# The last diagonal block of the attention scores: three reduced-precision passes in place of one full-precision matmul

## The reference

```python
qkv = silu(hidden @ qkv_w.T)              # 32 heads, q, k, v of 128 each
scores = einsum('bhnd,bhmd->bhnm', cq, ck) * diag_decay   # within a block of 32
intra  = einsum('bhnm,bhmd->bhnd', scores, cv)
inter  = einsum('bhnd,bhde->bhne', cq * q_decay, kv)      # kv carried from block to block
attn   = intra + inter                    # then RMS norm over all heads * norm_w
out1   = (sigmoid(hidden @ gate_w.T) * normed) @ out_w.T
```

## Time and profile before

| | |
|---|---|
| time, 3 runs | 1119.74, 1120.38 (median), 1122.15 us |
| the profiled execution | 1121.61 us, of which the span of its instructions is 1119.8 us |
| TensorE busy | 1085.3 us, 97% of the span, 5884 matmuls |
| weight loads busy | 944.8 us, 84% |
| DVE, ACT, POOL busy | 717.0, 683.6, 635.0 us (64%, 61%, 57%) |
| mean granted TensorE clock | 0.994 of full speed |

### The profile page before, as it was taken

How to read it: one execution, slowest core, us unless ns; L and a number is a source line. 1 busy time by engine, 2 the same in 40 slices (tenths; PEclk the granted TensorE clock), 3 DMA queues, 4 the chain that set the end, 5 groups by cost and what they waited for, 6 DMA issues and landing times.

```text
span 1119.8 us, 18930 instructions
## 1 busy us (share of the span) xinstructions
PE 1085.3 (97%) x5884; PEld 944.8 (84%) x5884; DVE 717.0 (64%) x1205; ACT 683.6 (61%) x1394; POOL 635.0 (57%) x617
## 2 busy tenths in 40 slices
PE   4999799999999999999999999999999999999997
PEld 3888588988889888988889888988889888888896
DVE  7767375575756667475766757566665757566666
ACT  6667365675656756575656756566566756567530
POOL 5837747376554846367473755458463765548620
PEclk9999899999999999999999999999999999999999
DMA  8213302021111101012020212011010211111122
GB/s 283 65 55 116 120 24 63 19 81 43 48 38 42 61 23 61 19 42 67 28 69 5 80 36 66 19 42 61 23 61 19 76 45 42 43 43 62 52 76 76
DMA packets 42805, 64.23 MB, mean 57 GB/s; under 512 B 3984, under 2 KB 21392, under 8 KB 42512
## 3 DMA queue, kind: packets, MB, share of 16 engines
q1 hardware_dynamic: 42480, 63.73, 17.8%
q10 hardware_dynamic: 288, 0.03, 0.0%
HBM read 54.84 MB, written 8.91 MB: 57 GB/s over the span
## 4 chain that ended last, share of the span: by engine, by line
PE 92%; DMA 2%; DVE 2%; issue 1%; POOL 1%; ACT 1%; SPq 0%; DVEq 0%; ACTq 0%; POOLq 0%
PE bank_q L1751 8%; PE bank_q L1753 8%; PE bank_q L1752 8%; PE bank_r L1752 5%; PE bank_r L1753 5%; PE bank_r L1751 5%; PE bank_p L1751 5%; PE bank_p L1753 5%; PE bank_p L1752 5%; PE outp L1753 5%; PE outp L1752 5%; PE outp L1751 5%; PE score L1753 3%; PE score L1752 3%; PE score L1751 3%; PE att L1753 3%
## 5 line engine op out<-in xcount | busy, mean ns | idle before, releaser
L413 POOL TENSOR_TENSOR w_lo<-combo,w_hi 128x768 fp32r<-128x768 f32 (+1 forms) x128 | 168.0, 1321 | 146.6 <-ACT w_hi L588 146.6
L413 POOL TENSOR_TENSOR w_lo<-raw,w_hi 128x256 fp32r<-128x256 f32 (+1 forms) x128 | 133.2, 1042 | 127.4 <-ACT w_hi L588 127.0
L450 POOL TENSOR_TENSOR sum_sq<-sum_sq,square 128x512 f32<-128x512 f32 x64 | 83.1, 1298 | 93.0 <-ACT square L731 92.9
L1326 DVE TENSOR_TENSOR acc<-acc,outp 128x512 f32<-128x512 f32 x116 | 79.5, 685 | 64.4 <-PE outp L1753 63.1
L1751 PE MATMUL bank_q<-c_hi,w_hi 128*128 128x512 f32 x276 | 110.3, 400 | 5.6 <-ACT ys L588 5.0
L1753 PE MATMUL bank_q<-c_hi,w_lo 128*128 128x512 f32 x276 | 108.9, 395 | 0.0
L1752 PE MATMUL bank_q<-c_lo,w_hi 128*128 128x512 f32 x276 | 108.7, 394 | 0.0
L1236 DVE TENSOR_TENSOR score<-score,table 128x512 f32<-128x512 f32 (+1 forms) x128 | 75.8, 628 | 42.7 <-PE score L1753 42.6
L588 ACT ACTIVATE p_hi<-score 128x896 fp32r<-128x896 f32 (+1 forms) x128 | 81.4, 650 | 35.6 <-DVE score L1236 33.2
L1751 PE MATMUL outp<-wo_hi,g_hi 128*128 128x512 f32 x252 | 100.4, 398 | 1.8 <-DVE acc L1324 1.8
L1184 DVE TENSOR_TENSOR xs<-bank_r,xs 128x512 f32<-128x512 f32 x64 | 44.2, 691 | 89.9 <-ACT xs L588 62.2
(11 more groups left out here) (268 smaller groups left out, 3450.5 us busy)
## 6 DMA issues: line engine op xcount, KB each, us to landing
raw<-w_chunks SPq DMA_DIRECT2D x165, 256.0 KB, 2.9
near_dram<-near SPq DMA_DIRECT2D x2, 2048.0 KB, 8.9
table<-near_dram SPq DMA_DIRECT2D x32, 128.0 KB, 2.0
acc<-x SPq DMA_DIRECT2D x8, 256.0 KB, 5.9
acc<-x SPq DMA_DIRECT2D x2, 1024.0 KB, 6.5
xb_dram<-acc SPq DMA_DIRECT2D x2, 1024.0 KB, 5.0
y<-xb_dram SPq DMA_DIRECT2D x8, 256.0 KB, 3.5
out<-acc SPq DMA_DIRECT2D x8, 256.0 KB, 2.2
```

The source lines that it names most:

```text
L413: pool.tensor_tensor(piece(w_lo[i % 2], j), piece_source(i, j), piece(w_hi[i % 2], j).bitcast(F32), ALU.subtract).then_inc(wlo[j], 1)
L450: pool.tensor_tensor(sum_sq[:, s % 2, :], sum_sq[:, s % 2, :], square[:], ALU.add).then_inc(summed, 1)
L1326: dve.tensor_tensor(tile, tile, outp, ALU.add).then_inc(acc_done, 1)
```

## The change

The scores of block j = 3 are computed by `three` like those of the other blocks, from the last 128 columns of `k_hi`, `k_lo`, `q_hi` and `q_lo`. `k_hi` and `k_lo` grow from 384 to 512 columns, and with them the silu, the high copy and the low subtraction of k. The tiles `q_last` and `k_last` and the instructions that fill them go, on ACT; `whole` remains for v alone, and the wait `scored` moves into `hi`. The order of everything else stays.

```diff
-                k_hi[b] = sb(f"k_hi{b}", [P, K_COLS], F32R, within)
-                k_lo[b] = sb(f"k_lo{b}", [P, K_COLS], F32R, within)
-                q_last[b] = sb(f"q_end{b}", [P, P], at=within)
-                k_last[b] = sb(f"k_end{b}", [P, P], at=within)
+                k_hi[b] = sb(f"k_hi{b}", [P, SEQ], F32R, within)
+                k_lo[b] = sb(f"k_lo{b}", [P, SEQ], F32R, within)
...
-                    cols = slice(0, SEQ if i == V1 or (i != V2 and ROW[c] == 0) else 256 if i == V2 else K_COLS)
+                    cols = slice(0, 256 if i == V2 else SEQ)
...
-                    elif ROW[c] == 1:
-                        made(i, c)
-                        scored(i, b)
-                        act.activation(k_last[b][:], banks[c][:, K_COLS:], ACT.Silu)
-                    else:
-                        act.wait_ge(silued[c], ev(g, i) + 1)
-                        scored(i, b)
-                        copy(q_last[b][:], banks[c][:, K_COLS:])
...
                     else:
+                        scored(i, b)
                         part = (q_hi if ROW[c] == 0 else k_hi)[b][:]
...
-                copy(q_last[b][:], bp[:, K_COLS:])
...
-                act.activation(bq[:, 0:K_COLS], bq[:, 0:K_COLS], ACT.Silu).then_inc(first_silu, 1)
-                act.activation(k_last[b][:], bq[:, K_COLS:], ACT.Silu)
+                act.activation(bq, bq, ACT.Silu).then_inc(first_silu, 1)
...
-                            pe.matmul(score23[:, P_LEN[2]:P_LEN[2] + P], k_last[b][:], q_last[b][:], start=True, stop=True,
-                                      skip_group_check=True).then_inc(s23, 1)
-                        else:
-                            to = score23[:, 0:P_LEN[2]] if j == 2 else score[:, j, 0:P_LEN[j]]
-                            three(to, k_hi[b][:, key], k_lo[b][:, key], q_hi[b][:, j * P:], q_lo[b][:, j * P:],
-                                  j < 2, True).then_inc(s23 if j == 2 else s01, 1)
+                        to = score[:, j, 0:P_LEN[j]] if j < 2 else score23[:, 0:P_LEN[2]] if j == 2 else score23[:, P_LEN[2]:P_LEN[2] + P]
+                        three(to, k_hi[b][:, key], k_lo[b][:, key], q_hi[b][:, j * P:], q_lo[b][:, j * P:],
+                              j != 2, True).then_inc(s01 if j < 2 else s23, 1)
```

More of the change, by code:

```diff
@@ L141, in build @@
         rs = sb("rs", [P, 4, NTB])
-        q_hi, q_lo, k_hi, k_lo, q_last, k_last, y = ([None] * BATCH for _ in range(7))
+        q_hi, q_lo, k_hi, k_lo, y = ([None] * BATCH for _ in range(5))
         for b in range(BATCH):
@@ L627, in whole @@
                     b = COL[c]
-                    if i == V2:
-                        made(i, c)
-                        at_least(act, att_ready, STEPS * (g - 1) + 4 * ROW[c] + 2 + b + 1)
-                        act.activation(v_last[ROW[c], b][:], banks[c][:, 256:512], ACT.Silu)
-                    elif ROW[c] == 1:
-                        made(i, c)
-                        scored(i, b)
-                        act.activation(k_last[b][:], banks[c][:, K_COLS:], ACT.Silu)
-                    else:
-                        act.wait_ge(silued[c], ev(g, i) + 1)
-                        scored(i, b)
-                        copy(q_last[b][:], banks[c][:, K_COLS:])
+                    made(i, c)
+                    at_least(act, att_ready, STEPS * (g - 1) + 4 * ROW[c] + 2 + b + 1)
+                    act.activation(v_last[ROW[c], b][:], banks[c][:, 256:512], ACT.Silu)
                 def hi(i, c):
@@ L785, in body @@
                     copy_u3(QK1)
-                    whole(QK1, "p")
                     weight(QK2, 2)
@@ L790, in body @@
                     silu(QK1, "q")
-                    whole(QK1, "q")
-                    whole(QK1, "x")
                     hi(QK1, "q")
@@ L796, in body @@
                     squares(1)
-                    whole(QK1, "r")
                     copy_m1(QK2)
@@ L810, in body @@
                     copy_u3(QK2)
-                    whole(QK2, "p")
                     weight(G23, 4)
@@ L816, in body @@
                     gated_hi(2)
-                    whole(QK2, "q")
                     silu(QK2, "x")
-                    whole(QK2, "x")
                     hi(QK2, "q")
@@ L831, in body @@
                     copy_u2(G23)
-                    whole(QK2, "r")
                     weight(QK3, 4)
@@ L848, in body @@
                     silu(QK3, "p")
-                    whole(QK3, "p")
                     probs01(4)
@@ L856, in body @@
                     silu(QK3, "x")
-                    whole(QK3, "x")
                     hi(QK3, "x")
@@ L863, in body @@
                     silu(QK3, "q")
-                    whole(QK3, "q")
                     weight(G01, 3)
@@ L868, in body @@
                     copy_m1(QK0)
-                    whole(QK3, "r")
                     weight(G01, 4)
@@ L1023, in body @@
                 silu(QK0, "p")
-                whole(QK0, "p")
                 copy_u3(QK0)
@@ L1030, in body @@
                 gated_hi(6)
-                whole(QK0, "q")
                 hi(QK0, "q")
-                whole(QK0, "x")
                 weight(NEXT + V1, 1)
@@ L1040, in body @@
                 weight(NEXT + V1, 2)
-                whole(QK0, "r")
                 weight(NEXT + V1, 4)
@@ L1088, in first_k @@
                 act.wait_ge(first_ready, TB * b + 2)
-                act.activation(bq[:, 0:K_COLS], bq[:, 0:K_COLS], ACT.Silu).then_inc(first_silu, 1)
-                act.activation(k_last[b][:], bq[:, K_COLS:], ACT.Silu)
+                act.activation(bq, bq, ACT.Silu).then_inc(first_silu, 1)
                 act.wait_ge(first_silu, 2 * b + 2)
-                copy(k_hi[b][:], bq[:, 0:K_COLS]).then_inc(first_high, 1)
+                copy(k_hi[b][:], bq).then_inc(first_high, 1)
             def first_gates(b, h):
@@ L1704, in first_lows @@
                 dve.wait_ge(first_high, 2 * b + 2)
-                dve.tensor_tensor(k_lo[b][:], bq[:, 0:K_COLS], k_hi[b][:].bitcast(F32), ALU.subtract).then_inc(first_low, 1)
+                dve.tensor_tensor(k_lo[b][:], bq, k_hi[b][:].bitcast(F32), ALU.subtract).then_inc(first_low, 1)
             def combo_lo(k, n):
```

## The result

The changed kernel takes 1127.37 us (median of 4 runs, 1126.98 to 1128.47), the kernel before, run beside it, 1121.27 us (4 runs, 1119.74 to 1122.9): a ratio of 1.006, 95% interval 1.0045 to 1.0076. The profiled execution took 1128.47 us, 1126.6 of them its span, so the span grew by 6.8 us. The medians of four grew by 6.1 us; the interval of the ratio allows 5.0 to 8.5.

A forecast was written before the change was run, and what follows sets the result against it. TensorE alone was taken to bound the loop: 0.336 - 0.225 = +0.111 us a step, times 62 steps = +6.9 us, so 1121.61 became 1128.5 us profiled, 1127.3 us as median; range 1119.0 to 1132.0 us.

The forecast's parts named there:

- The bound: Loop on TensorE: busy for all 129.08 us of a period, so only what TensorE gains or loses reaches the total.
- Price of the pass: New 128-column `fp32r` matmuls in the scores: each costs its weight load, 0.112 us, so three cost 0.336 us a step.
- The Trainium skill's 81 ns: Scores on TensorE: 81 ns per load and matmul pair would give +0.018 us a step, +1.1 us in all.
- Price of the old pair: Full-precision matmul removed from the scores: two records by two weight loads, taken as 0.225 us a step.
- Steps that count: Two of 64 steps lie before first-body waits that do not end with them; 62 x 0.111 = +6.9 us.
- the wait for `p_lo` in the last body: TensorE's 0.3 us wait at the end, behind DVE instructions: grows by +0.13 us at most, counted in the range.
- ACT: Copies and silu of q and k on ACT: net -0.35 us a step, -22 us, no effect on the total.
- DVE: Low part of k on DVE: +0.13 us a step, 8.5 us in all, inside 47 us free per period.
- the copy to `ys`: Behind DVE's slowest low part of k (1.80 us): 1.5 us of room before TensorE needs it, enough for 0.6 us more.
- The clock: First body, 126 to 135 us, mean granted clock 0.62: half-clock stretch may shorten or lengthen, about 2 us either way.

The follow-up runs named there:

- e1: Kernel after, with the last score block again by one full-precision matmul, from k_hi and q_hi alone: 1120.77 us.
- e4: Kernel before, with its ACT and DVE work, but the last score block by three reduced passes (stand-in third key block): 1128.45 us.
- e3: Kernel after, with the three passes of the last score block over its upper 64 query columns alone, same three weight loads: 1127.14 us.
- e7: Kernel after without the last block of the scores: 1108.49 us in one run.
- e6: Kernel after with the three passes of the last score block done twice: 1145.78 us in one run.
- e5: Kernel after, with the three narrow passes of the last score block alternating with the three 512-column passes of the first: 1128.69 us.

## Why the prediction was right

- *The bound.* Right. The period grew by what TensorE was given, and e1 and e4 put all of it there.
- *Price of the pass: 0.112 us, from the one-column matmuls of the earlier trace rows.* Right: 0.111, whatever the columns (e3). That the load sets it was my reason, and it is the likely one, not a shown one. The Trainium skill's 81 ns for a pair of load and 128-column matmul (TensorE: Matmul & The Clock Gate, "Back-to-back issue gap") doesn't hold for these `fp32r` operands, which take 111. By the Trainium skill's rule for a load, columns divided by 1.2 GHz (TensorE: Matmul & The Clock Gate, "LDWEIGHTS (loading the stationary operand)"), 128 columns take an estimated 107 ns, near the 111 measured.
- *Price of the old pair: 0.225 us.* A little too high: 0.210 over the period. I read it from starts around the block, and the matmuls behind it are not quite the same with and without it: the first two of 512 columns there take 0.226 and 0.232 us, and 0.229 and 0.233 in e7. So a step costs +0.124, not +0.111.
- *Steps that count: 62 of 64.* Right for the first body: four of its first six steps lengthen the way to the next one, by 0.09 to 0.13 us each, and two, as counted, give nothing or can't be seen. Even so the seventh scores step comes only 0.10 us later (161.08 to 161.18), because this execution began 0.08 us earlier and was 0.30 us shorter in the stretch of waits behind the fourth step. That stretch takes from 34.5 to 36.4 us in the traces at hand, so this part is chance. The six periods from there gave 6 x 0.993 = 5.96. The last ten steps gave 0.75 in place of 1.24: I had the wait for `p_lo` in the last body growing by 0.13 at most, and it went, which alone gave back 0.48 us. So the step was priced too low, by 62 x 0.013 = 0.8 us, and 0.9 us that I had not counted came off; the 6.9 forecast and the 6.8 measured agree so closely by luck. The median is luck too: the kernel before had 1121.27 us beside the kernel after, not the 1120.38 that I started from.

The seventh scores step of the first body, in the kernel before and in the kernel after:

```profile
161.08 0.48 PE L1751 MATMUL score<-q_hi,k_hi 128*128 128x512 f32 x1
```
```profile
161.18 0.48 PE L1711 MATMUL score<-q_hi,k_hi 128*128 128x512 f32 x1
```

- *ACT: -22 us, no effect.* The effect was right, the size was not: -10.8 us. Added up one by one ACT's durations fell by 23.6 us (770.1 to 746.5), as forecast. But they overlap those of their neighbours, and the busy time counts such a stretch once.
- *DVE: +8.5 us, no effect.* It rose by 10.2. The subtractions for `k_lo` gave 7.5 of it (from `xs` 29.6 to 32.8 us, from the bank 17.1 to 21.1, at the start 1.1 to 1.4). DVE's durations added up rose by 8.2; the rest is less overlap between its instructions. I named the stretch behind the slowest subtraction but the wrong reader: I checked the copy to `ys`, with 1.5 us of room, while an output tile waits for DVE's sum before that, with about 0.5. In e1 that room is used up in three bodies, by up to 0.26 us, but also in single bodies of e3 (0.43) and e6 (0.19), where TensorE has as much to do as in the kernel after, or more. In the one trace of the kernel after it never is. Nothing was lost there, but the margin that I stated was not the smallest.
- *The clock.* The half-clock stretch of the first body didn't change here (0.62 from 126 to 135 us in both). It can: in e4 the stretch from 118 to 126 us was at 0.60 instead of 1.00, and that execution was 1.2 us longer than the one of the kernel after at the same period, 1.1 of them before the seventh scores step.

Busy times by stretch, e4:

```profile
118.00:126.00 8.00, 6.05 (x16) 4.32 (x17) 2.23 (x4) 1.24 (x3) 7.92 (x8) 0.60 0.53 168
```

## What to carry to other kernels

In a row of matmuls with a new stationary tile each, a reduced-precision float32 pass cost 0.111 us here at 128 columns and at 64, by all signs for its weight load. So three passes pay off only when the columns are many enough to hide it: at 128 columns one full-precision instruction (0.21 us) beats three passes (0.33), at 256 it loses (0.42 to 0.345). To price a matmul form in a loop that TensorE fills, compare whole periods, not starts around it. When an instruction on a covered engine grows, look for the earliest reader behind it, not the most striking one.

## What had not been expected

- The full-precision pair costs 0.210 us at 128 columns and about 0.42 at 256, proportional to the columns. At 128 that is a little less than two passes (0.222), though it has two loads. Within the block it isn't: in the kernel before the pair starts at 291.47, and the matmul behind it, whose successor's load starts with it, at 291.70, so 0.22 us for two loads. The 0.012 us less come out of the matmuls behind, which differ by a few ns with and without the block; why was not settled.

```profile
291.47 0.38 PE L1811 MATMUL score<-q_end,k_end 128*128 128x128 f32 x2
291.58 0.19 PEld L1751 LDWEIGHTS score<-q_hi,k_hi 128*128 128x128 f32 x1
291.70 0.19 PEld L1752 LDWEIGHTS score<-q_lo,k_hi 128*128 128x128 f32 x1
```

- In all twelve traces, some 5,800 to 6,100 matmuls each, no load of the next stationary operand starts before the record of the current matmul, also where wide passes would leave time (e5).
- Half as many columns in a narrow pass give 0.001 us a pass (e3).
